# A transformer layer with three sublayers on one core: the order of the prologue, and queries as three fp32r products

## What is computed

```python
q = (query @ Wq + bq).reshape(b, s, NUM_HEADS, KEY_SIZE)      # query = layernorm(x)
k = (key @ Wk + bk).reshape(b, key.shape[1], NUM_HEADS, KEY_SIZE)
v = (value @ Wv + bv).reshape(b, value.shape[1], NUM_HEADS, VALUE_SIZE)
logits = jnp.einsum('bshd,bShd->bhsS', q, k) / np.sqrt(KEY_SIZE).astype(np.float32)
weights = jax.nn.softmax(logits, axis=-1)
attn = jnp.einsum('bhsS,bShd->bshd', weights, v).reshape(b, s, NUM_HEADS * VALUE_SIZE)
return attn @ Wo + bo
```

## Time and profile before

| | us |
|---|---|
| median of three runs | 1481.84 (1481.35 to 1483.1) |
| the profiled execution | 1481.26 |
| its span in the profile | 1479.5 |
| TensorE busy | 1425.7 (96%) |
| VectorE busy | 753.0 (51%) |
| ACT busy | 487.3 (33%) |
| GpSimd busy | 199.4 (13%) |
| mean granted clock of TensorE | 0.983 of 2.4 GHz |

### The profile page before, as it was taken

One profiled execution on the slowest core, in us unless ns is written; L12 is line 12 of the kernel. 1 busy time (PEld: TensorE's weight loads), 2 busy tenths in 40 slices (PEclk: granted clock), 3 DMA queues, 4 the chain that ended last, 5 costly groups with the idle time before them and its releaser, 6 DMA issues.

```text
span 1479.5 us, 22668 instructions
## 1 busy us (share of the span) xinstructions
PE 1425.7 (96%) x8596; PEld 1116.0 (75%) x8596; DVE 753.0 (51%) x1776; ACT 487.3 (33%) x1101; POOL 199.4 (13%) x164
## 2 busy tenths in 40 slices
PE   5999999999999999999999999999999888789999
PEld 4667778777877877787778777777787666678877
DVE  5335543463345335633543364345434646877769
ACT  3115531372144115611541273135213624222110
POOL 2321100130020003200100031011000333300030
PEclk9999999999999999999999999999999998799999
DMA  6511100150021003200200141011001320113200
GB/s 214 164 50 29 33 22 1 54 150 12 0 62 28 12 1 116 89 12 3 77 22 1 46 133 36 1 54 36 12 1 40 115 87 29 58 53 119 95 19 29
DMA packets 45817, 78.33 MB, mean 53 GB/s; under 512 B 6688, under 2 KB 14912, under 8 KB 44688
## 3 DMA queue, kind: packets, MB, share of 16 engines
q1 hardware_dynamic: 44192, 72.38, 15.8%
q0 software_dynamic: 1520, 4.51, 0.9%
HBM read 71.63 MB, written 5.24 MB: 52 GB/s over the span
## 4 chain that ended last, share of the span: by engine, by line
PE 91%; DVE 4%; issue 1%; ACT 1%; DMA 1%; SPq 1%; POOL 0%; ACTq 0%; DVEq 0%
PE b_ps L1123 24%; PE b_ps L1101 24%; PE b_ps L483 9%; PE b_ps L1170 8%; PE b_ps L1139 7%; PE b_ps L1152 7%; PE b_ps L509 3%; PE b_ps L414 3%; PE b_ps L1111 2%; PE b_ps L1195 2%; DMA stage<-in_ctx 1%; PE b_ps L419 1%; ACT b_ctxT L1230 1%; PE b_ps L1163 0%; ACT t_prob L553 0%
## 5 line engine op out<-in xcount | busy, mean ns | idle before, releaser
L1123 PE MATMUL b_ps<-b_ctxT,wk 128*128 128x512 f32 x1536 | 390.0, 402 | 0.0
L1101 PE MATMUL b_ps<-wv,b_ctxT 128*128 128x512 f32 x1536 | 372.2, 401 | 11.2 <-DVE b_ctxT L1309 11.2
L1101 PEld LDWEIGHTS b_ps<-wv,b_ctxT 128*128 128x128 f32 x1536 | 288.9, 190 | 87.6 <-issue 22.4
L1123 PEld LDWEIGHTS b_ps<-b_ctxT,wk 128*128 128x128 f32 x1536 | 281.5, 188 | 86.8 <-issue 25.0
L1286 ACT COPY b_pT<-b_ps 128x512 f32<-128x512 f32 x128 | 75.0, 586 | 603.4 <-PE b_ps L1152 602.8
L1404 DVE COPY b_pT<-b_ps 128x512 f32<-128x512 f32 x128 | 88.3, 690 | 254.3 <-PE b_ps L1152 254.1
L1322 DVE COPY b_V<-b_ps 128x512 f32<-128x512 f32 x128 | 88.5, 692 | 247.3 <-PE b_ps L1101 247.3
L1280 ACT ACTIVATE b_prob<-b_prob,b_negm 128x512 f32<-128x512 f32 x256 | 182.9, 720 | 58.9 <-DVE b_negm L1425 58.9
L1419 DVE TENSOR_SCALAR_CACHE_REDUCE b_prob<-b_ps 128x512 f32<-128x512 f32 x256 | 166.5, 688 | 29.6 <-PE b_ps L1139 28.4
L1061 POOL TENSOR_TENSOR wk<-stage,wk 128x512 fp32r<-128x512 f32 x30 | 39.0, 1300 | 763.4 <-ACT wk L1238 763.4
L1152 PE MATMUL b_ps<-ident,b_prob 128*128 128x128 f32 x1024 | 133.5, 273 | 3.9 <-DVE b_pT L1404 3.6
(11 more groups left out here) (192 smaller groups left out, 1111.6 us busy)
## 6 DMA issues: line engine op xcount, KB each, us to landing
stage<-in_ctx SPq DMA_DIRECT2D x64, 256.0 KB, 2.9
b_wo<-in_Wo SPq DMA_DIRECT2D x8, 1024.0 KB, 5.7
stage<-in_Wk SPq DMA_DIRECT2D x30, 256.0 KB, 2.6
stage<-in_Wv SPq DMA_DIRECT2D x28, 256.0 KB, 3.2
b_q<-q_s SPq DMA_DIRECT2D x32, 128.0 KB, 3.1
stage<-in_self_w SPq DMA_DIRECT2D x16, 256.0 KB, 2.7
t_raw<-in_q_proj SPq DMA_DIRECT2D x16, 256.0 KB, 4.5
t_raw<-in_k_proj SPq DMA_DIRECT2D x16, 256.0 KB, 3.5
```

The costliest lines, as they stand in the source:

```text
L1101: mm = nc.tensor.matmul(ps[:, G.bank[item]], ctxT[:, a, k, n * P:(n + 1) * P], wv[:, w, k], start=m == 0, stop=m == len(terms) - 1)
L1123: mm = nc.tensor.matmul(ps[:, G.bank["k", t]], wk[:, i % 2, w, k], ctxT[:, a, k, s * BANK:(s + 1) * BANK], start=m == 0, stop=m == len(ter ...
```

## The change

The prologue's order becomes v0 v1 v2 v3 x v4 v5 q0 v6 q1 v7 v8 q2 and so on, and it ends in v15 q7. SP loads x ahead of ctx1, and ctx1 to ctx5 ahead of wq; wq and Wk follow, then ctx6 to ctx15. The four blocks of transposes go to banks 3, 4, 5 and 6, one each. The turned x is split as it leaves PSUM: ACT writes `xhi`, VectorE `xlo` (over `xn`, block by block). Each query weight is split on ACT (`query_weight`) and VectorE (`query_rest`) into one of two buffers, those of queries 0 and 1 with the item x, the others two queries ahead. A query is 12 fp32r products. `xlo` lies by blocks of tokens, so the moving operand of its four products is four pieces of 128 columns. ACT and VectorE wait for the last stores of the queries only ahead of the first turned probabilities, no longer ahead of the first keys.

```diff
-        for j, chunks in enumerate(((0, 1, 2), (3, 4), (5,), (6, 7), (8,), (9, 10), (11,), (12, 13), (14,), (15,))):
...
+        for item in "v0 v1 v2 v3 x v4 v5 q0 v6 q1 v7 v8 q2 v9 q3 v10 v11 q4 v12 q5 v13 v14 q6 v15 q7".split():
...
-        xnT = at("xnT", [P, C, TOK], prob_at + 4 * C * HW + 4 * NB * D)
+        xhi = at("xhi", [P, C, TOK], prob_at + 4 * C * HW + 4 * NB * D, F32R)
+        xlo = at("xlo", [P, NB, D], prob_at + 4 * C * HW, F32R)
+        wq_parts = at("wq_parts", [P, 2, 2, C, P], kst_at, F32R)
...
@@ SP
-            for n in range(2):
-                load(("ctx", 0, n))
+            load(("ctx", 0, 0))
             for b in range(NB):
                 sp.dma_start(xs[:, b], x[b]).then_inc(x_in[b], 16)
-            for n in range(2, 4):
+            for n in range(1, 6):
                 load(("ctx", 0, n))
             for c in range(C):
                 sp.dma_start(wq[:, c], Wq[:, c]).then_inc(wq_in[c], 16)
             for i in range(2):
                 sp.dma_start(raw[C + i], Wk[i]).then_inc(pre_in[C + i], 16)
-            for n in range(4, NC):
+            for n in range(6, NC):
                 load(("ctx", 0, n))
@@ TensorE
-                        if b >= 2:
-                            pe.wait_ge(xT_done, b - 1)
                         for c in range(C):
-                            mm = nc.tensor.transpose(ps[:, TB + b % 2, c * P:(c + 1) * P], xn[:, b, c * P:(c + 1) * P], ident[:])
+                            mm = nc.tensor.transpose(ps[:, SCB + b, c * P:(c + 1) * P], xn[:, b, c * P:(c + 1) * P], ident[:])
...
-                        for c in range(C):
-                            pe.wait_ge(wq_in[c], 16)
+                    pe.wait_ge(wq_lo, j + 1)
                     if j >= 2:
                         pe.wait_ge(qlo_done, j - 1)
-                    for c in range(C):
-                        mm = nc.tensor.matmul(ps[:, SCB + j % 2, :TOK], wq[:, c, j * P:(j + 1) * P], xnT[:, c, :],
-                                              start=c == 0, stop=c == C - 1)
+                    terms = [(w, a, c) for w, a in ((0, 0), (0, 1), (1, 0)) for c in range(C)]
+                    for m, (w, a, c) in enumerate(terms):
+                        mm = nc.tensor.matmul(ps[:, SCB + j % 2, :TOK], wq_parts[:, j % 2, w, c],
+                                              xlo[:, :, c * P:(c + 1) * P] if a else xhi[:, c].rearrange("p (b t) -> p b t", b=NB),
+                                              start=m == 0, stop=m == len(terms) - 1)
@@ ACT
+            def query_weight(j):
+                if j == 0:
+                    for c in range(C):
+                        act.wait_ge(wq_in[c], 16)
+                if j >= 2:
+                    act.wait_ge(q_psum, j - 1)
+                nc.scalar.copy(wq_parts[:, j % 2, 0], wq[:, :, j * P:(j + 1) * P]).then_inc(wq_hi, 1)
...
+                    for b in range(NB):
+                        act.wait_ge(xT_psum, b + 1)
+                        nc.scalar.copy(xhi[:, :, b * P:(b + 1) * P], ps[:, SCB + b].rearrange("p (c t) -> p c t", c=C)
+                                       ).then_inc(xhi_done, 1)
+                    for j in range(2):
+                        query_weight(j)
                     for n in range(C, len(PRE)):
                         pre_split(n)
+                    for n in (6, 7):
+                        split_hi(("ctx", 0, n))
-                elif item[0] == "v" and item[2] + 4 < NC:
+                elif item[0] == "v" and item[2] + 4 < NC and item[2] not in (2, 3):
...
-            for i in range(QBUFS):
-                act.wait_ge(q_stored[i], 32 * (NP // QBUFS))
...
+                    if w == 0:
+                        for n in range(QBUFS):
+                            act.wait_ge(q_stored[n], 32 * (NP // QBUFS))
@@ VectorE
+            def query_rest(j):
+                dve.wait_ge(wq_hi, j + 1)
+                nc.vector.tensor_tensor(wq_parts[:, j % 2, 1], wq[:, :, j * P:(j + 1) * P], wq_parts[:, j % 2, 0].bitcast(F32),
+                                        ALU.subtract).then_inc(wq_lo, 1)
...
-                        dve.wait_ge(xT_psum, b + 1)
-                        nc.vector.tensor_copy(xnT[:, :, b * P:(b + 1) * P],
-                                              ps[:, TB + b % 2].rearrange("p (c t) -> p c t", c=C)).then_inc(xT_done, 1)
+                        dve.wait_ge(xhi_done, b + 1)
+                        nc.vector.tensor_tensor(xlo[:, b].rearrange("p (c t) -> p c t", c=C), ps[:, SCB + b].rearrange("p (c t) -> p c t", c=C),
+                                                xhi[:, :, b * P:(b + 1) * P].bitcast(F32), ALU.subtract).then_inc(xT_done, 1)
+                    for j in range(2):
+                        query_rest(j)
                     for n in range(C, len(PRE)):
                         pre_rest(n)
+                    chunk_rest(0, 6)
```

More of the change, by code:

```diff
@@ L137, in __init__ @@
         self.first = []
-        for j, chunks in enumerate(((0, 1, 2), (3, 4), (5,), (6, 7), (8,), (9, 10), (11,), (12, 13), (14,), (15,))):
[L139 to L143, removed]
+        for item in "v0 v1 v2 v3 x v4 v5 q0 v6 q1 v7 v8 q2 v9 q3 v10 v11 q4 v12 q5 v13 v14 q6 v15 q7".split():
+            self.first.append(("v", 0, int(item[1:])) if item[0] == "v" else ("q", int(item[1:])) if item[0] == "q" else ("x",))
         ring = [x for x in self.first if x[0] == "v"]
@@ L934, in layer @@
         xT_psum, xT_done, xbo_done = sem("xT_psum"), sem("xT_done"), sem("xbo_done")
+        xhi_done, wq_hi, wq_lo = sem("xhi_done"), sem("wq_hi"), sem("wq_lo")
         q_psum, qhi_done, qlo_done = sem("q_psum"), sem("qhi_done"), sem("qlo_done")
@@ L1265, in _ @@
                                          ).then_inc(qhi_done, 1)
+                    if j + 2 < NP:
+                        query_weight(j + 2)
             act.wait_ge(bias_in, 32)
-            for i in range(QBUFS):
-                act.wait_ge(q_stored[i], 32 * (NP // QBUFS))
             for t in range(LAST + 1):
@@ L1359, in _ @@
                     value_out(item)
-                    if item[2] + 4 < NC and item[2] % 2 == 0:
+                    if item[2] + 4 < NC and item[2] % 2 == 0 and item[2] != 2:
                         chunk_rest(0, item[2] + 4)
@@ L1373, in _ @@
                                                    qhi[:, j % QBUFS].bitcast(F32), ALU.add, ALU.subtract).then_inc(qlo_done, 1)
+                    if j + 2 < NP:
+                        query_rest(j + 2)
             dve.wait_ge(bias_in, 32)
-            for i in range(QBUFS):
-                dve.wait_ge(q_stored[i], 32 * (NP // QBUFS))
             for t in range(LAST + 1):
@@ L1401, in _ @@
                     dve.wait_ge(t_psum, 2 * w + 2)
+                    if w == 0:
+                        for n in range(QBUFS):
+                            dve.wait_ge(q_stored[n], 32 * (NP // QBUFS))
                     if 2 * w >= SLOTS:
```

## The result

| | before | after |
|---|---|---|
| median | 1482.47 us (4 runs) | 1469.66 us (1468.7 to 1471.33, 4 runs) |
| profiled execution | 1481.26 us | 1469.58 us |
| its span | 1479.5 us | 1467.8 us |
| TensorE busy | 1425.7 us | 1417.4 us |

The ratio of after to before is 0.992, with a 95% interval of 0.9907 to 0.9933: 12 us faster by the ratio and 12.8 us by the medians, where 10.9 were forecast. The time lies in the range. A later series of five runs of the same kernel, on another occasion, gave 1470.77 us and a ratio of 0.993 (0.9918 to 0.9942).

The account below looks back on a forecast made before the run. TensorE, busy 1425.7 of 1479.5 us, was taken as the bound. Gains of 6.7 and 5.1 us, less a 1.2 us wait, with 0.3 of rounding and hand-overs, gave 10.9 us: 1470.9 us, range 1468.9 to 1473.8.

Parts of the forecast that it names:

- Step 1: First transposes in the prologue: TensorE's 4.50 us stall and the half-speed clock after it go, 6.7 us gained.
- Step 2: Queries: twelve fp32r products replace four full-precision ones, 0.64 us less for each of eight queries, 5.1 us gained.
- the lower bound: Price of an xlo query product: 0.233 us, as for a contiguous operand; the upper end was full precision's 0.858 us.
- third rival: Queries: xlo products cost as much as full-precision ones, 20 us more over eight queries, 1490.9 us; chance 0.03.
- fifth rival: Queries: products run at 0.214 us, a query takes 2.57 us, 1.8 us less over eight, 1469.1 us; chance 0.04.
- Step 3: Value chunk 1: its load lands later, at 14.4 us, so TensorE waits 1.2 us for it (nothing to 1.9 us).
- the 13 us of the lower bound: Chunk 1's load may land at 13 us, with fewer bytes in flight behind it, making TensorE's wait nothing.
- Step 4: Prologue: added copies and subtractions on ACT and VectorE lie beside TensorE and cost nothing; tightest spare room 1.4 us.
- second rival: Prologue loads: wq, ctx5 or ctx6 land later than 30.7 us, perhaps 2 us lost, 1473 us; chance 0.06.
- the first: Rival at chunk 1's wait and the transposes: the clock falls after all, 2.2 us, 1473.1 us; chance 0.10.
- The sum: Whole prologue: keys start at 82.5 us instead of 93.45, 10.9 us gained; execution 1470.4 us, median 1470.9 us.
- fourth rival: After the prologue: the earlier start of the keys is given back, 1481.8 us; chance 0.03.

Follow-up runs that it names:

- both edits in the old order: The kernel before with four banks for the transposes and fp32r queries, item and load order kept as before; 1470.38 us, ratio 0.993.
- The run with added products: The changed kernel plus 24 full-precision 128x128 products of the identity with itself ahead of chunk 0, whose results are unused; 1470.46 us, ratio 0.9931.
- two banks: The changed kernel with the old two transpose banks and the wait for their copies back; 1471.07 us, ratio 0.9936.

## Why the prediction was right

**Step 1, the stall and the slow clock (6.7 us): right in size, half right in cause.** The banks alone gave 6.9 us from the first transposes to the keys. The prediction put the removal down to the banks and to chunks 4 and 5 being issued ahead of wq. The second is not needed (both edits in the old order equal the changed kernel), and the loads alone lose 4 us.

**Step 2, the queries (5.1 us): right, a little small.** They gave 8 x (3.43 - 2.73) = 5.6 us. An xlo product with its moving operand in four pieces takes 389 ns in the records like every other, so the lower bound was the right one and the third rival, slower than before, falls. The chain's 0.228 us for a product (2.73/12) lies between the trace's 0.233 that I took and the 0.216 that the Trainium skill's page "TensorE: Matmul & The Clock Gate", section "Back-to-back issue gap", gives for the gap of an isolated product. The measurement agrees with neither exactly, and the fifth rival (2.57 us) falls.

**Step 3, the wait of 1.2 us for chunk 1: right for chunk 1, and it cost nothing that was not lost already.** Chunk 1 was forecast to start at 16.6 us and started at 16.83. But TensorE was not idle ahead of it: chunk 0 began 0.80 us late, as the last load of Wv landed at 9.80 us, and took 4.83 us where 4.20 were forecast, because the slow start was longer. It ended at 16.79 us, 1.43 us later than forecast, just as chunk 1 became ready. So the sum had nearly the right total, 1.2 us, in the wrong column, and that is luck. The run with added products shows the wait itself, 1.71 us, inside the bounds of nothing and 1.9 us. In the runs with that load order ACT's copy of ctx1 started at 14.00 to 14.69 us (15.23 in the run with the loads alone, where Wv was late too). None came near the 13 us of the lower bound, and they lie close to the 14.4 + 0.1 by the order of the ring that the Trainium skill's "DMA: Bandwidth & Descriptors", section "Queues, rings and completion order", describes. Whether fewer bytes behind it gained some tenths of a microsecond stays open.

**Step 4, the work beside TensorE: right.** TensorE waits for no query weight and no xlo after. The second rival (late loads) falls with it, and so does the first: the clock stood at 1.00, and not even the waits of 1.06 us (two banks) or 1.71 us (added products) were followed by a clock of 0.50.

**The sum: the keys within 0.1 us, the profiled execution 0.8 us too late, the median 1.2 us.** Part of the first figure is luck too. Query 0 began at 32.77 us where 32.3 was forecast, and the queries, 0.06 us shorter each than forecast, gave back the same 0.5 us. The fourth rival, a gain given back, falls: behind the keys the two profiles of the changed kernel take 1385.2 and 1386.8 us, the one of before 1386.0. The distance of the median, 1469.66 us against 1470.9, is of the size of this scatter, and the later series gave 1470.77 us. By its time alone the result does not tell the forecast from the fifth rival's 1469.1 us; the length of a query does.

## What to carry to other kernels

When an in-order engine stalls on a buffer, ask first whether one more buffer lets it go on with other work: here two more PSUM banks gave what a new order of items and loads was meant to give, and the order gave nothing on top. A load moved ahead moves another one back, so look at what stands behind it in the consumer's list: VectorE's subtraction of chunk 6 made the same load order a loss of 4 us. Count from a point behind the scatter: from the first transposes to the keys the two profiles of the changed kernel and the four with the same work in that stretch agree within 0.03 us (57.32 to 57.35), while their medians differ by 2.5 us. And a wait that was forecast but does not show may lie under something else; remove that, and it comes up.

## What the runs showed of the hardware

- The records of the granted clock do not show the slow first products. A window of one microsecond in the changed kernel, and then one in the kernel before, where the first products were over:

```profile
13.00:14.00 1.00, 1.00 (x4) 1.00 0.87 330
```

```profile
15.00:16.00 1.00, 1.00 (x6) 1.00 1.03 422
```

  Both are told as 1.00, but the first has four products of 512 columns under way and the second six. By the start times in the traces one product follows the other by 427 ns in the first stretch, as it does in 28.6 to 30.8 us of before, where the record says 0.50 (1.2 GHz); behind it they follow by about 231 ns. With TensorE working since 3.72 us the same twelve products took 3.03 us in place of 4.83. So the first stretch has to be read from the start times or the durations. In the eleven profiles without added products it lasts for some 7 to 14 products.
- The last of the four loads of Wv was picked up by ACT anywhere from 8.45 to 11.05 us, with the same loads ahead of it. On a kernel whose first product hangs on it that is scatter of 2 us, which one profile of each kernel does not average out.
- The stall of 6.21 us in the run with the loads alone was followed by a clock of 0.50, as the one of 4.50 us was before and the one of 3.52 us with the queries alone (0.50 in 29.00 to 32.00 us); those of 1.06 and 1.71 us were not.
